# Vision tower in one kernel: in the heads stage, image b + 2 is normalized and transposed inside step b instead of behind it

## The reference, cut to what matters

```python
h = tokens(x)                                  # (8 images, 1030 rows, 192)
h = h + retention(_layernorm(h))
h = h + experts(_layernorm(h))
h = h + latent_attention(_layernorm(h), ...)   # its first part is the stage at hand
h = h + mixture(_layernorm(h))

def latent_attention(x, Wq, Wkv, ...):         # 12 heads of 16
    q, kv = _rope(_heads(x @ Wq)), _rope(_heads(x @ Wkv))
    lkv = _ln(kv)                              # over the 16 of each head; the values
    ...                                        # softmax(q kv^T / 4) lkv, projection
```

## Time and profile before

| what | value |
|---|---|
| median of 3 runs | 4367.64 us (4366.02 to 4367.65) |
| the profiled execution: its own time | 4368.69 us |
| its span, first to last instruction | 4367.0 us |
| mean granted TensorE clock, share of full speed | 0.943 |
| heads stage, stretch of the span | 1735 to 2051 us |

### The profile page before, as it was taken

One profiled execution on the slowest core, in us unless ns is written; L12 is line 12 of the kernel. 1 busy time (PEld: TensorE's weight loads), 2 busy tenths in 40 slices (PEclk: granted clock), 3 DMA queues, 4 the chain that ended last, 5 costly groups with the idle time before them and its releaser, 6 DMA issues. The chain is left out here.

```text
span 4367.0 us, 74345 instructions
## 1 busy us (share of the span) xinstructions
PE 3881.2 (89%) x23713; PEld 2315.3 (53%) x23715; DVE 2457.6 (56%) x4592; ACT 1506.8 (35%) x2993; POOL 1294.1 (30%) x1502
## 2 busy tenths in 40 slices
PE   8899778799999997664999999999996888899998
PEld 8788555466666665432233333333332455577776
DVE  1566469522222222785887787778772437644444
ACT  0222114211111111342477777777774221011111
POOL 0222004244444443465000001000001002177776
PEclk9999999899999998776799999999998999999999
DMA  6221111332332221346333333333315432267775
GB/s 225 65 64 52 32 41 41 103 63 63 63 63 63 63 63 22 102 132 147 47 46 46 46 46 53 50 57 46 46 27 136 122 96 42 70 161 173 175 171 123
DMA packets 335828, 353.98 MB, mean 81 GB/s; under 512 B 52332, under 2 KB 297123, under 8 KB 334127
## 3 DMA queue, kind: packets, MB, share of 16 engines
q1 hardware_dynamic: 251999, 268.42, 25.4%
q0 software_dynamic: 61248, 61.98, 9.1%
q10 hardware_dynamic: 22416, 21.19, 1.7%
HBM read 241.18 MB, written 110.47 MB: 81 GB/s over the span
## 5 line engine op out<-in xcount | busy, mean ns | idle before, releaser
L2131 DVE TENSOR_REDUCE at_mx<-psum 128x1 f32<-128x998 f32 (+1 forms) x768 | 884.9, 1190 | 252.0 <-PE psum L1955 251.6
L2086 ACT ACTIVATE at_p<-psum 128x512 f32<-128x512 f32 (+3 forms) x1536 | 851.9, 588 | 300.0 <-PE psum L2029 270.5
L2029 PE MATMUL psum<-at_q,at_k 99*128 99x512 bf16 (+3 forms) x1536 | 521.4, 382 | 20.4 <-issue 15.4
L1955 PE MATMUL psum<-at_k,at_q 96*128 96x512 bf16 (+3 forms) x1536 | 475.9, 393 | 69.1 <-POOL at_identb L1911 31.7
L2015 PE MATMUL psum<-at_p,at_v 128*32 128x486 f32 (+3 forms) x3072 | 408.3, 604 | 1.0 <-ACT at_p L2086 0.7
L1256 ACT ACTIVATE ex_silu<-psum 128x384 f32<-128x384 f32 (+1 forms) x288 | 131.8, 458 | 768.2 <-PE psum L1200 637.9
L2029 PEld LDWEIGHTS psum<-at_q,at_k 99*128 99x128 bf16 (+1 forms) x1536 | 155.5, 102 | 427.4 <-ACT at_p L2086 275.2
L1287 DVE TENSOR_TENSOR ex_hT<-ex_silu,psum 128x384 f32<-128x384 f32 (+1 forms) x288 | 147.5, 512 | 416.2 <-ACT ex_silu L1256 270.7
L1917 POOL DMA_DIRECT2D recips<-at_shares x24 | 12.8, 533 | 1039.9 <-DVE at_mx L2131 723.8
L1222 PE MATMUL psum<-ex_wd,ex_hT 128*128 128x192 f32 (+1 forms) x1728 | 291.5, 327 | 0.0
L1955 PEld LDWEIGHTS psum<-at_k,at_q 96*128 96x128 bf16 (+1 forms) x1536 | 152.2, 105 | 231.9 <-DVE at_mx L2131 66.7
(11 more groups left out here) (393 smaller groups left out, 7038.8 us busy)
## 6 DMA issues: line engine op xcount, KB each, us to landing
mx_wd<-in_e_dT SPq DMA_DIRECT2D x72, 288.0 KB, 3.9
qk_parts<-hd_parts SPq DMA_DIRECT2D x32, 579.4 KB, 3.8
at_k<-qk_parts SPq DMA_DIRECT2D x144, 128.8 KB, 5.0
at_q<-qk_parts SPq DMA_DIRECT2D x144, 124.8 KB, 4.5
tok_p<-in_x SPq DMA_DIRECT2D x12, 1176.0 KB
mx_wg<-in_e_gT SPq DMA_DIRECT2D x72, 192.0 KB, 2.4
mx_wu<-in_e_uT SPq DMA_DIRECT2D x72, 192.0 KB, 2.7
v_rows<-hd_v_out SPq DMA_DIRECT2D x8, 1536.0 KB
```

Source lines behind the costliest of these rows:

```text
L1955: mm = pe.matmul(psum[0:ctx_rows[t], 3 + 2 * ((PRO + n) % 2) + k, 0:w], Q[v][0:R6, j * 1024 + 128 * t:j * 1024 + 128 * t + ctx_rows[t]], K ...
L2029: pe.matmul(psum[0:n, i % RING, 0:w], K[u][:, j, 128 * t:128 * t + n], Q[u][:, j * 1024 + at:j * 1024 + at + w], start=True, stop=True).th ...
L2086: act.activation(P[0:n, c % 2, j, 0:w], psum[0:n, i % RING, 0:w], ACT.Exp).then_inc(exp_ready, 1)
L2131: dve.tensor_reduce(mx[0:ctx_rows[t], j * CT + t:j * CT + t + 1], pair(n)[0:ctx_rows[t], 0:CTX], AX_X, ALU.max).then_inc(s_free, 1)
```

## The change

`hd_rows` and `hd_xnT` are given up. The rows go to a buffer that a later stage has already reserved (`lent[2]`), and the turned rows to two such buffers (`lent[0]`, `lent[1]`), one for even images and one for odd ones. `hd_cen` gets two halves. In step b the pieces of work on image b + 2 move from behind tile 8 into the tiles: statistics and their root after tile 1, normalizing after tile 3, transposes (0, 1), (2, 3), (4, 5) and the ScalarE copies at tiles 5, 6 and 7. The square moves from ahead of tile 0 to tile 1. On VectorE, `turn(b + 1, 0)` now comes ahead of the mean and the deviations of image b. VectorE's wait for `v_ready` moves from ahead of the deviations to ahead of the reciprocal L1714. Nothing in SyncE's list differs.

```diff
-def phase_heads(nc, psum, inp, y, qk_parts, v_rows, ident, ident_in, consts, consts_in, first, loaded, v_loaded):
+def phase_heads(nc, psum, inp, y, qk_parts, v_rows, ident, ident_in, consts, consts_in, first, loaded, v_loaded, lent):
...
-        rows = sb("hd_rows", [128, KT + 1, D])
+        rows = lent[2]
-        xnT = sb("hd_xnT", [DP, DC, SEQ])
+        xnT = [a[0:DP] for a in lent[0:2]]
...
-        cen = sb("hd_cen", [128, NH, DH])
+        cen = sb("hd_cen", [128, 2, NH, DH])
...
-        VAR, ROOT = 3, 5
+        SQUARE, VAR, ROOT = 1, 3, 5
+        STATS, NORM, TURNS = 1, 3, {5: (0, 1), 6: (2, 3), 7: (4, 5)}
...
# TensorE, step
                 for t, a, r in TILES:
                     if following:
-                        project(b + 1, t, a, r, False)
+                        project(b + 1, 1 - half, t, a, r, False)
                     for j in due(t):
                         turn_back(b, half, j)
-                if following > 1:
-                    turn_rows(b + 2)
+                    for k in TURNS.get(t, ()) if following > 1 else ():
+                        turn_rows(b + 2, k)
...
# ScalarE
-            def step(b, following=True):
-                act.wait_ge(cen_ready, b + 1)
-                act.activation(square[:], cen[:], ACT.Square).then_inc(sq_ready, 1)
+            def step(b, half, following=True):
                 for t in range(NT):
                     for j in due(t):
                         first_part(b, j)
                         if j:
                             second_part(b, j - 1)
+                    if t == SQUARE:
+                        act.wait_ge(cen_ready, b + 1)
+                        act.activation(square[:], cen[:, half], ACT.Square).then_inc(sq_ready, 1)
+                        if following:
+                            root(b + 2)
                     if t == VAR:
                         act.wait_ge(var_ready, b + 1)
                         act.activation(vstd[:], var[:], ACT.Sqrt, scale=1.0 / DH, bias=eps[:]).then_inc(vstd_ready, 1)
+                    for k in TURNS.get(t, ()) if following else ():
+                        take_xnT(b + 2, half, k)
                 second_part(b, NB_R - 1)
-                if following:
-                    root(b + 2)
-                    take_xnT(b + 2)
...
# VectorE
             def step(b, half, following=2):
                 kv = rot[:, half, :, D:NQ].rearrange("p t (h d) -> p t h d", h=HEADS)
+                if following:
+                    turn(b + 1, 0, 128, False)
                 dve.wait_ge(rot_ready, b * NT + NT)
                 dve.tensor_reduce(mean[:].rearrange("p (t h) -> p t h", t=NT), kv, AX_X, ALU.add).then_inc(v_mean, 1)
                 dve.wait_ge(v_mean, b + 1)
                 dve.tensor_scalar(mean[:], mean[:], 1.0 / DH, None, ALU.mult).then_inc(v_scaled, 1)
                 dve.wait_ge(v_scaled, b + 1)
-
-                dve.wait_ge(v_ready, b)
-                dve.tensor_tensor(by_tile(cen[:]), kv, wide(mean[:]), ALU.subtract).then_inc(cen_ready, 1)
+                dve.tensor_tensor(by_tile(cen[:, half]), kv, wide(mean[:]), ALU.subtract).then_inc(cen_ready, 1)
                 for t, _, n in TILES:
-                    if following:
+                    if following and t:
                         turn(b + 1, t, n, False)
                     for j in due(t):
                         remainder(b, j)
+                    if t == STATS and following > 1:
+                        spread_of(b + 2)
+                    if t == NORM and following > 1:
+                        norm(b + 2)
                     if t == VAR:
                         dve.wait_ge(sq_ready, b + 1)
                         dve.tensor_reduce(var[:], square[:], AX_X, ALU.add).then_inc(var_ready, 1)
                     if t == ROOT:
                         dve.wait_ge(vstd_ready, b + 1)
+
+                        dve.wait_ge(v_ready, b)
                         dve.reciprocal(vrstd[:], vstd[:]).then_inc(vrstd_ready, 1)
-                if following > 1:
-                    normalize(b + 2)
```

More of the change, by code:

```diff
@@ L1554, in _, with turn_rows, project @@
             pe.wait_ge(consts_in, HEADS_CONSTS)
[L1556 to L1569, removed]
+            def turn_rows(b, k):
+                m, (at, n) = k // 3, CUTS[k % 3]
+                tiles = [x for x in TILES if at <= x[1] < at + n]
+                pe.wait_ge(xn_ready, b * NT + (tiles[-1][0] + 1))
+                pe.wait_ge(xT_ready, b * NB_X + max(k - 1, 0))
+                for t, a, r in tiles:
+                    last = pe.transpose(psum[0:DP, k % 2, a - at:a - at + 128], xn[:, t, m * DP:(m + 1) * DP], ident[:])
+                last.then_inc(xT_full, 1)
+            def project(b, half, t, a, r, first):
                 if t == 0:
@@ L1628, in root, with take_xnT @@
                 act.activation(std[:], mv[:, :, 1], ACT.Sqrt, bias=eps[:]).then_inc(ln[2], 1)
[L1630 to L1637, removed]
-            def step(b, following=True):
-                act.wait_ge(cen_ready, b + 1)
-                act.activation(square[:], cen[:], ACT.Square).then_inc(sq_ready, 1)
+            def take_xnT(b, half, k):
+                m, (at, n) = k // 3, CUTS[k % 3]
+                if k == 0 and (not isinstance(b, int) or b > 1):
+                    act.wait_ge(qk_full, b * NT - NT)
+                act.wait_ge(xT_full, b * NB_X + (k + 1))
+                act.activation(xnT[half][:, m, at:at + n], psum[0:DP, k % 2, 0:n], ACT.Identity).then_inc(xT_ready, 1)
+            def step(b, half, following=True):
                 for t in range(NT):
@@ L1649, in step @@
                         act.activation(vstd[:], var[:], ACT.Sqrt, scale=1.0 / DH, bias=eps[:]).then_inc(vstd_ready, 1)
+                    for k in TURNS.get(t, ()) if following else ():
+                        take_xnT(b + 2, half, k)
                 second_part(b, NB_R - 1)
[L1651 to L1653 removed]
             for b in range(2):
                 root(b)
[L1657 to L1659 removed]
+                for k in range(NB_X):
+                    take_xnT(b, b, k)
+            with act.Fori(0, B // 2 - 1) as i:
+                for half in range(2):
+                    step(i * 2 + half, half)
             for b in (B - 2, B - 1):
[L1661 removed]
+                step(b, b % 2, False)
         @block.vector
@@ L1665, in _, with spread_of, norm @@
             dve.wait_ge(set_up, SETUP)
-            def normalize(b):
+            def spread_of(b):
                 dve.wait_ge(rows_in, b * 32 + 32)
+                for t, _, n in TILES:
+                    last = dve.bn_stats(stats[0:n, t, :], rows[0:n, t, :])
+                last.then_inc(ln[0], 1)
+                dve.wait_ge(ln[0], b + 1)
+                dve.memset(pad[:], 0.0)
+                for t, _, n in TILES:
+                    last = dve.bn_aggr(mv[0:n, t, :], stats[0:n, t, :])
+                last.then_inc(ln[1], 1)
+            def norm(b):
+                dve.wait_ge(ln[2], b + 1)
+                dve.reciprocal(rstd[:], std[:]).then_inc(ln[3], 1)
+                dve.wait_ge(ln[3], b + 1)
                 dve.wait_ge(xT_full, b * NB_X)
-                layernorm_tiles(dve, b, rows, xn, (stats, mv, std, rstd, pad), ln, xn_ready)
+                for t, _, n in TILES:
+                    dve.tensor_scalar(xn[0:n, t, :], rows[0:n, t, :], mv[0:n, t, 0:1], rstd[0:n, t:t + 1],
+                                      ALU.subtract, ALU.mult).then_inc(xn_ready, 1)
             def turn(b, t, n, first):
@@ L1721, in _ @@
                 turn(0, t, n, True)
-            normalize(1)
+            spread_of(1)
+            norm(1)
             with dve.Fori(0, B // 2 - 1) as i:
```

18 lines of the change are left out of this document (11 added, 7 removed).

## The result

The changed kernel takes 4403.25 us in the median of 4 runs (4399.82 to 4406.95), the kernel before 4366.83: a ratio of 1.0083, 95% interval 1.0070 to 1.0095. The forecast was 4386.5, range 4372 to 4402. The direction and the two mechanisms are there, but the cost is nearly twice the 18.9 us that were worked out, and the median lies 1.25 us above the range. The kernel before also scatters more than the 0.04% given at the start: over all runs it took 4359 to 4385 us.

The account below looks back on a forecast made before the run. VectorE was taken to pace the heads stage. Cycles of 29.6 + 8.6 = 38.2 us, with a one-time loss at the start, gave +18.9 on 4368.69, 4387.6; the median lies 1.05 lower: 4386.5 us, range 4372 to 4402.

Parts of the forecast that it names:

- The rows behind the store: SyncE loads image b + 2 behind the values' store, so VectorE waits 4 us at the statistics in steps 1 to 5.
- E to the next S by the rows: From the end of scaled values to the next statistics, set by the rows' arrival: 8.6 us, range 8.4 to 9.6.
- The coupling at tiles 5 to 8: Transposes waiting for ScalarE's copies delay TensorE's projections and so turns 7 and 8: 2.0 us, between 0 and 3.
- The rival of the low clock: TensorE at half speed at tiles 7, 8 and next 0: 26 us more in all, 4413; chance 0.10.
- Statistics and norm: The statistics and normalizing moved into VectorE's tiles, costing 3.15 us and 2.86 us, plus 0.6 for the collision.
- the collision: VectorE's normalizing meets a GpSimd add or third_part: 0.6 us a step; paid in full 1.2, 4390.1, chance 0.08.
- S to E: From the start of a step's statistics (S) to the end of its scaled values (E): 29.6 us, bounds 28.0 to 31.0.
- The sum: Heads stage: first S, five cycles of 38.2 us, a last S to E; mean of step 7 at 2031.3, +18.9 us.
- The first S: Start of the first moved statistics, after the first turn, mean and deviations: claimed at 1788.9.
- The signs: Trace marks of a right forecast: 4 us gaps at statistics, steps 37 to 40 us apart, turns 7 and 8 waiting.
- Faster, or the rows in time: Rows arrive within 4.55 us of E, all is hidden: period 32.2 us, 13 us less, 4354.5; chance 0.06.
- The uncoupled case: Copies at tiles 6 to 8 delay nobody, 0 in place of 2.0 us: total +6.9 us; chance 0.20.

Follow-up runs that it names:

- run 1: The changed kernel with SyncE issuing the load of image b + 3 ahead of the store of the values: 4382.39 us, ratio to before 1.0029.
- run 4: The changed kernel with extra transposes filling TensorE's idle time at tiles 4 and 6: ratio to the kernel before 1.0045.
- 10: The changed kernel with the early load of run 1 and the filled TensorE of run 4: ratio to the kernel before 0.9988.
- run 2: The changed kernel with the six groups of transposes and six copies back behind tile 8, load still late: ratio to the kernel before 1.0036.
- run 3: The changed kernel with both the early load of run 1 and the transposes and copies behind tile 8 of run 2: ratio to before 0.9998.
- run 5: Run 3 with the first turn of a step back behind the mean and deviations on VectorE: ratio to the kernel before 0.9974.
- run 9: Run 5 with GpSimd scaling the values one step later, behind its job 0: ratio to the kernel before 0.9974.
- 7: The changed kernel with early load, all six transposes and copies under norm and variance, and values scaled one step later: ratio to before 0.9984.
- run 11: Run 9 with SyncE loading the next stage's first operands behind the stores of image 5 instead of image 6: ratio to before 0.9963.

## Why the prediction was wrong in size and right in cause

- **The rows behind the store: right, and somewhat under-sized.** Waits of 4.4 to 5.0 us in steps 1 to 5 and none in step 0 were there, and run 1 takes 22.5 us away with them alone. The term "E to the next S by the rows" had 8.6 us with bounds of 8.4 to 9.6; 9.5 in four steps and 10.1 in one were measured. In the earlier trace rows the last bytes had moved by 7.8 us behind E; in the changed kernel they still move in 1870 to 1871, up to 8.7 us behind it, and VectorE starts 0.8 us later. The prediction held that the earlier issue of the load changes nothing. Here it is issued 1.5 us behind E in place of 2.7, so that rows and values are under way together for longer. Whether that makes the transfers slower is open.
- **The coupling at tiles 5 to 8: right as a mechanism, mis-sized; this is the step that failed.** The prediction put it at 2.0 us, with `turn` 8 at 1908.05 in place of 1906.08. Measured from the end of job 8 (1888.56 in the changed kernel, 1901.44 before) to `turn` 8 it is 8.2 us against 4.6: 3.5 us. The excess is the clock. The term counted tile 7's projection at 1.46 us, and TensorE, which stands still for the copies, ran it at 1.2 GHz in 2.77. With the full clock in runs 4 and 10 the same distance is 6.3 and 6.1 us, a coupling of 1.7 and 1.4 us: the 2.0 were fair for the order alone. The rival of the low clock described this place with 4.4 us a step and a chance of 0.10; its price was too large, since only one of its three projections was slow where it mattered. Run 4 puts the price at 1.9 us a step. Forecast and rival were no alternatives: the order takes TensorE's lead away, and only then does the low clock cost anything, as run 2 shows.
- **Statistics and norm: right.** 3.1 us (1871.83 to the `turn` at 1874.91) against 3.15, and 3.73 us (1878.92 to 1882.65) against 3.46, of which 0.87 is the collision that was put at 0.6. The wait at tile 3 is 0.70, not 0.40.
- **S to E together:** 31.3 to 31.5 us (31.7 in step 0) against 29.6. With the rows 40.9 a cycle against 38.2.
- **The sum.** The first S was 1789.18 against 1788.9. The mean of step 7 came 17.6 us later than worked out: 0.3 at the first S, 14.3 in the five cycles (5 of them by the rows, 9 by S to E), 1.9 in the last S to E and 1.2 in what follows, where the deviations cost 2.63 in place of 1.96. That they would be slowed was missed; the sum used for them.
- **The signs.** The waits at the statistics, the first `turn` of a step (0.9 to 1.2 us of waiting) and the scaling of the mean (1.3 to 1.7 us) came as named. The marks lie 40.8 to 41.8 us apart and not 37 to 40, `turn` 8 mostly waits 0.7 us and not 1, and four L1576 of tile 7 took 2.77 us, the sign that the prediction had given for the clock.
- **Faster, or the rows in time:** its deciding point was 4.55 us; the rows needed 9.5. Refuted by the trace, and by run 3 also the hope behind it: with the rows in time and the order repaired, the step is 34.2 us and not 32.2, since behind tile 8 VectorE waits 4.4 us for the six copies and the projection of the next image.
- **The uncoupled case** (0 for the coupling, +6.9 us) is refuted by run 2's 3.4 us a step.
- **What normalizing in the midst is worth.** Nothing by itself: run 3 against the kernel before, 34.2 us against 35.05 a step, given back in the one-time loss at the first step. With the mean first (run 5) it is worth 6 us of stage, with the values later (run 9) 11, of which 2 lie ahead of the loop by the clock.

Not tried: a spare pair of banks, which would let TensorE transpose without waiting for a copy, since all eight are in use.

## What to carry to other kernels

Work that is moved to an earlier point needs its inputs earlier: follow its load back through the queue that issues it, and measure from the event that the load stands behind, not from its own duration. Here a single place in SyncE's list was worth 22 us, more than the 17 us by which the best of these kernels shortens the stage of the kernel before.

A piece put into the midst of two in-order lists that feed each other (TensorE and ScalarE in this kernel) cost not its length but the lead that one had on the other. Such a lead also hides a low clock of TensorE: with it the slow projection cost nothing (run 2), without it 1.9 us a step (run 4).

## What the runs showed of the hardware

- VectorE's deviations, with two inputs in SBUF, take 2.63 us in place of 1.96 where GpSimd's `add` starts just before them, as at 1862.26 in the changed kernel. The Trainium skill (SBUF — State Buffer, Who interferes with whom) says that a VectorE instruction with two SBUF inputs contends with a GpSimd instruction that reads SBUF; the 0.67 us agree, and where GpSimd has nothing to do at that moment (runs 2, 3, 5, 7 and 9) it is 1.96 again. The statistics, with one input, were never lengthened beside GpSimd's 3.1 us in run 9 (2.42 us).
- TensorE, at a granted clock of 1.00 until 1887, worked 0.6 us between 1884.4 and 1888 and was at 0.50 (1.2 GHz) from 1888 to 1894; with extra transposes ahead of it (run 4) tile 7's projection ran at 1.00.
- The same work ahead of the loop had the clock at 1.00 in one stretch of 4 us in runs 4 and 9 and at 0.50 to 0.53 in all others; the mean of step 0 then came 4.4 us (run 4) and 3.2 us (run 9 against run 11) earlier.
- Values and rows, 2.3 MB in one queue, took 9.5 to 10.1 us from the end of the computation to use. The Trainium skill (DMA: Bandwidth & Descriptors, Anatomy of one DMA) would have it near 7.4 by my estimate from its fit, which it gives for transfers issued by GpSimd, while SyncE issues these; the measurement decides.
